# A two-layer transformer block on one core: 122 positions of its time table changed

## What is computed

```python
xn = layernorm(x)
# layer 0: latent attention and a mixture of experts
lat = layernorm(xn @ W_dkv) * gamma + beta          # latent of 32
q, k, v = rope(xn @ W_q), rope(lat @ W_uk), lat @ W_uv   # 16 heads of 8
a = causal_softmax(q @ k.T / sqrt(8)) @ v @ W_o
gates = softmax(top2_of_8(xn @ Wg + bg))
f = sum(gates[e] * (relu(xn @ W1[e] + b1[e]) @ W2[e] + b2[e]) for e in range(8))
x = x + a + f
xn = layernorm(x)
# layer 1: three attentions mixed, and a feed-forward with four matrices
mod = sigmoid(xn @ cg_W + cg_b + cons_vec @ am_W + am_b)     # one per head
ctx = 0.3 * softmax(mod * (q1 @ k1.T) / sqrt(8)) @ v1 + 0.7 * mha(xn, ca, 4 heads)
ctx = 0.85 * ctx + 0.15 * mha(ctx, mc, 4 heads)
h = silu(xn @ w1) * (xn @ w2)
f = gelu(gelu(h @ h1) @ h2) @ w3
x = x + ctx @ Wo + f
```

## Time and profile before

| What | Value |
|---|---|
| Time, three runs | 1737.87, 1743.94, 1736.77 us; median 1737.87 |
| Profiled execution | span 1744.8 us, 34024 instructions |
| PE busy | 1542.1 us (88%), 11497 matmuls |
| PE weight loads (beside matmuls) | 656.0 us (38%) |
| DVE busy | 1199.4 us (69%) |
| ACT busy | 1055.2 us (60%) |
| POOL busy | 792.1 us (45%) |
| Transfers | 159.35 MB, mean 91 GB/s |

### The profile page before, as it was taken

How to read it: one execution, slowest core, us unless ns; L and a number is a source line. 1 busy time by engine, 2 the same in 40 slices (tenths; PEclk the granted TensorE clock), 3 DMA queues, 4 the chain that set the end, 5 groups by cost and what they waited for, 6 DMA issues and landing times.

```text
span 1744.8 us, 34024 instructions
## 1 busy us (share of the span) xinstructions
PE 1542.1 (88%) x11497; PEld 656.0 (38%) x11497; DVE 1199.4 (69%) x3135; ACT 1055.2 (60%) x2322; POOL 792.1 (45%) x725
## 2 busy tenths in 40 slices
PE   3586898999999999998999999999999999889878
PEld 1353453245333543345333543345324533232232
DVE  7554478567875788667885788677876677476523
ACT  2372475667656765676666765677657765636442
POOL 5246345535645456354644455354644461501120
PEclk9998699999999999999999999999999999989877
DMA  7652451136212631136212621145212620201010
GB/s 277 205 153 69 135 158 36 57 109 176 63 34 77 167 102 48 63 115 159 63 34 87 180 79 52 62 135 145 58 46 82 186 78 7 62 15 35 1 37 6
DMA packets 138875, 159.35 MB, mean 91 GB/s; under 512 B 15744, under 2 KB 100304, under 8 KB 137808
## 3 DMA queue, kind: packets, MB, share of 16 engines
q1 hardware_dynamic: 134608, 148.79, 29.4%
q0 software_dynamic: 4096, 8.40, 1.6%
HBM read 115.96 MB, written 40.85 MB: 90 GB/s over the span
## 4 chain that ended last, share of the span: by engine, by line
PE 61%; DVE 13%; ACT 9%; issue 6%; POOL 6%; DMA 3%; SPq 2%; ACTq 0%; POOLq 0%; DVEq 0%
PE banks L454 58%; DVE negmax L879 6%; ACT probs L1222 3%; ACT hm L1291 3%; POOL psums L1443 2%; POOL xslots L1417 1%; DMA qkc<-relm 1%; DVE h L1103 1%; ACT L1222 1%; PE banks L731 1%; POOL halves L1399 1%; PE banks L684 1%; SPq L1579 1%; ACT h L1340 1%; POOL yg L1432 0%
## 5 line engine op out<-in xcount | busy, mean ns | idle before, releaser
L1222 ACT ACTIVATE probs<-banks 128x512 f32<-128x512 f32 (+3 forms) x1216 | 582.1, 535 | 371.7 <-PE banks L454 352.9
L879 DVE TENSOR_REDUCE negmax<-banks 128x1 f16<-128x512 f32 x768 | 492.2, 685 | 159.5 <-PE banks L454 156.5
L875 DVE CUSTOM_DVE_ANT_0 scr<-banks,mask_row 128x384 bf16<-128x384 f32 (+3 forms) x512 | 230.2, 487 | 150.9 <-PE banks L454 149.1
L454 PE MATMUL banks<-kp,qs 32*128 32x512 f16 (+3 forms) x1024 | 239.7, 360 | 60.4 <-DVE negmax L875 23.5
L454 PE MATMUL banks<-probs,vp 128*32 128x512 f32 (+3 forms) x2048 | 241.0, 544 | 0.2 <-POOL probs L1395 0.2
L454 PE MATMUL banks<-qs,kp 32*128 32x512 f16 (+3 forms) x1024 | 218.5, 352 | 23.2 <-ACT probs L1222 15.9
L1483 POOL TENSOR_TENSOR h_lo<-h,h_hi 128x512 f16<-128x512 f32 x96 | 114.4, 1209 | 246.4 <-ACT h_hi L1334 150.8
L1423 POOL TENSOR_TENSOR hl<-hm,hh 128x512 f16<-128x512 f32 x120 | 139.7, 1166 | 131.7 <-DVE hh L1045 131.7
L1291 ACT ACTIVATE hm<-banks,wt 128x128 f32<-128x128 f32 x480 | 137.8, 374 | 77.4 <-PE banks L454 77.0
L454 PE MATMUL banks<-qkc 97*128 97x512 f16 (+1 forms) x512 | 168.5, 402 | 8.7 <-DVE negmax L879 3.0
L454 PEld LDWEIGHTS banks<-kp,qs 32*128 32x128 f16 x1024 | 63.1, 92 | 277.5 <-DVE negmax L879 109.8
(11 more groups left out here) (212 smaller groups left out, 2462.0 us busy)
## 6 DMA issues: line engine op xcount, KB each, us to landing
wt<-wexp SPq DMA_DIRECT2D x120, 258.0 KB, 3.1
wt<-wexp SPq DMA_DIRECT2D x120, 256.0 KB, 3.0
qkc<-relm SPq DMA_DIRECT2D x96, 128.0 KB, 3.2
qs<-relq SPq DMA_DIRECT2D x64, 128.0 KB, 2.3
kp<-relk SPq DMA_DIRECT2D x64, 128.0 KB, 2.3
relm<-halves SPq DMA_DIRECT2D x32, 256.0 KB, 2.1
xg<-xslots SPq DMA_DIRECT2D x24, 256.0 KB, 3.0
yslots<-yv SPq DMA_DIRECT2D x24, 256.0 KB, 3.6
```

The source lines that it names most:

```text
L454: return nc.tensor.matmul(psum[rows_, bank, cols_], lhsT, rhs, start=start, stop=stop)
L875: v.tensor_tensor_reduce(scr[:, s, 0:kw], psum[:, SCO + s, 0:kw], mask_row[:, T - kw:T], -1.0, 3e38, ALU.add, ALU.min, negmax[:, g.n % 2, ...
L879: v.tensor_reduce(negmax[:, g.n % 2, NC * h + c:NC * h + c + 1], psum[:, SCO + s, 0:kw], AX.X, ALU.max, negate=True).then_inc(sem("max"), 1)
L1222: a.activation(keys(g, c)[:, 2 * pair + s, q0:T], psum[:, TRA + s, q0:T], ACT.Exp, scale=SCALE[main(g)]).then_inc(sem("exp"), 1)
```

## The change

122 of the 311 positions in the table change, most by one to three slots, some by more (`x_load` by nine, the last of `spread0`, the query sum and `mc_spread` by six). No step is added or removed, and every wait stays, with its count renumbered from the table. The order inside a slot's body is the same. Two of the last batch's fillers now have positions 767 and 768, behind the end of the loop. The diff is whole, without its header:

```diff
@@ -80,8 +80,9 @@
 PLAN += [("a1", "mid", at, gr) for gr, at in enumerate((120, 128, 136))] + [("a1", "last", 152, NG - 1), ("mc", "tail", 224, 0)]
 A1_AT = (120, 128, 136, 152)
 
-MOVE = {"route": {0: 6}, "warm0": {-1: -6}, "warm1": {-1: 6}, "front": {}, "keys": {0: -8, 1: -5}, "joined": {0: 3}, "prep": {0: 13},
-        "ca": {-1: -24}, "mid": {-1: -24}, "last": {-1: -30}, "ffn": {-1: -24}, "tail": {-2: -12, -1: -52}}
+MOVE = {"route": {0: 6, 1: -1}, "warm0": {-2: 1, -1: -6}, "warm1": {2: 1, -2: -1, -1: 6}, "front": {}, "keys": {0: -8,
+        1: -5}, "joined": {0: 3}, "prep": {0: 13}, "ca": {-1: -24}, "mid": {-1: -24}, "last": {-1: -30}, "ffn":
+        {-1: -24}, "tail": {-2: -12, -1: -52}}
 
 
 @dataclass
@@ -113,57 +114,57 @@
     return out
 
 
-AT = {"l1_split": 14, "x_load": -59, "x_stat": -50, "x_root": -49, "x_norm": -48, "xT0": -39, "xT0_out": -38, "xr_hi": -43,
-      "xr_lo": -42, "lat": -36, "lat_stat": -36, "lat_root": -34, "lat_norm": -33, "latT": -33, "latT_out": -32, "q0": -34,
-      "q0_out": -33, "q0r": -32, "q0r_out": -31, "q0_sum": -30, "q0_send": -27, "k0": -19, "k0_out": -18, "k0r": -16,
-      "k0r_out": -15, "k0_sum": -15, "k0_send": -12, "rank0": -35, "rank1": -32, "rank2": -33, "gex": -33, "gates": -29,
-      "pos": -29, "starts": -27, "slots": -25, "addresses": -25, "pick": -10, "v0a": 3, "v0a_out": 4, "v0b": 30,
-      "v0b_out": 29, "gT": 39, "gT_out": 40, "back0": 53, "back0_out": 54, "wo0": 57, "wo0_out": 58, "x1_stat": 63,
-      "x1_root": 65, "x1_norm": 66, "xT1": 67, "xT1_out": 69, "xl1": 72, "cg": 71, "cg_out": 71, "mod": 72, "q1": 73,
-      "q1_out": 75, "q1_low": 75, "q1_send": 76, "k1": 75, "k1_out": 76, "k1_low": 75, "k1_send": 78, "caq": 77,
-      "caq_out": 78, "caq_low": 79, "caq_send": 80, "cak": 79, "cak_out": 79, "cak_low": 82, "cak_send": 82,
-      "ca_spread": 109, "cav": 112, "cav_out": 113, "v1": 129, "v1_out": 130, "bo": 100, "ca_div": 136, "ca_mul": 141,
-      "ca_o": 143, "ca_o_out": 145, "gelu1": 151, "gelu2": 166, "f3": 171, "f3_out": 173, "f3_add": 172, "back1": 181,
-      "ctx": 181, "mcq": 205, "mcq_out": 205, "mcq_low": 207, "mcq_send": 209, "mck": 208, "mck_out": 209, "mck_low": 210,
-      "mck_send": 213, "mc_spread": 217, "mcv": 220, "mcv_out": 221, "mc_div": 249, "mc_mul": 250, "mc_o": 254,
-      "mc_o_out": 255, "ctx2": 256, "wo1": 256, "wo1_out": 256, "store": 257}
-AT.update({("spread0", i): at for i, at in enumerate((-7, -5, 5, 17), 0)})
-AT.update({("spread1", i): at for i, at in enumerate((110, 117, 126, 142), 0)})
+AT = {"l1_split": 15, "x_load": -50, "x_stat": -46, "x_root": -46, "x_norm": -45, "xT0": -39, "xT0_out": -38, "xr_hi": -44,
+      "xr_lo": -40, "lat": -36, "lat_stat": -36, "lat_root": -35, "lat_norm": -33, "latT": -33, "latT_out": -32, "q0":
+      -34, "q0_out": -33, "q0r": -32, "q0r_out": -31, "q0_sum": -24, "q0_send": -25, "k0": -19, "k0_out": -18, "k0r":
+      -16, "k0r_out": -16, "k0_sum": -15, "k0_send": -11, "rank0": -35, "rank1": -32, "rank2": -33, "gex": -33,
+      "gates": -27, "pos": -27, "starts": -27, "slots": -25, "addresses": -24, "pick": -11, "v0a": 3, "v0a_out": 3,
+      "v0b": 31, "v0b_out": 30, "gT": 39, "gT_out": 40, "back0": 53, "back0_out": 54, "wo0": 57, "wo0_out": 58,
+      "x1_stat": 63, "x1_root": 65, "x1_norm": 66, "xT1": 67, "xT1_out": 69, "xl1": 66, "cg": 72, "cg_out": 72, "mod":
+      74, "q1": 73, "q1_out": 74, "q1_low": 75, "q1_send": 76, "k1": 75, "k1_out": 75, "k1_low": 76, "k1_send": 78,
+      "caq": 77, "caq_out": 78, "caq_low": 80, "caq_send": 79, "cak": 79, "cak_out": 79, "cak_low": 81, "cak_send":
+      81, "ca_spread": 106, "cav": 112, "cav_out": 113, "v1": 129, "v1_out": 131, "bo": 100, "ca_div": 136, "ca_mul":
+      141, "ca_o": 143, "ca_o_out": 144, "gelu1": 152, "gelu2": 166, "f3": 171, "f3_out": 173, "f3_add": 171, "back1":
+      181, "ctx": 181, "mcq": 205, "mcq_out": 205, "mcq_low": 207, "mcq_send": 208, "mck": 208, "mck_out": 209,
+      "mck_low": 210, "mck_send": 209, "mc_spread": 211, "mcv": 220, "mcv_out": 222, "mc_div": 249, "mc_mul": 250,
+      "mc_o": 254, "mc_o_out": 255, "ctx2": 256, "wo1": 256, "wo1_out": 257, "store": 257}
+AT.update({("spread0", i): at for i, at in enumerate((-6, -5, 8, 23), 0)})
+AT.update({("spread1", i): at for i, at in enumerate((106, 117, 127, 143), 0)})
 AT.update({("h0", i): at for i, at in enumerate((28, 36, 43, 51), 0)})
 AT.update({("h0_out", i): at for i, at in enumerate((28, 37, 44, 52), 0)})
-AT.update({("h1", i): at for i, at in enumerate((151, 157, 166, 179), 0)})
-AT.update({("h1_out", i): at for i, at in enumerate((152, 157, 167, 180), 0)})
-AT.update({("up", i): at for i, at in enumerate((9, 12, 13, 16, 17, 20, 22, 24, 25, 29, 30, 32, 34, 35, 38), 0)})
-AT.update({("down", i): at for i, at in enumerate((13, 15, 17, 19, 21, 23, 25, 27, 31, 32, 33, 35, 37, 39, 42), 0)})
-AT.update({("wup", i): at for i, at in enumerate((5, 7, 7, 10, 12, 15, 17, 19, 21, 25, 25, 25, 29, 31, 33), 0)})
-AT.update({("wdn", i): at for i, at in enumerate((9, 11, 13, 15, 17, 19, 21, 23, 25, 27, 29, 31, 33, 35, 37), 0)})
-AT.update({("scatter", i): at for i, at in enumerate((-16, -15, -16, -15), 0)})
-AT.update({("gather", i): at for i, at in enumerate((45, 46, 48, 49), 0)})
-AT.update({("xg_load", i): at for i, at in enumerate((-5, -4, 7, 19), 0)})
+AT.update({("h1", i): at for i, at in enumerate((147, 157, 166, 179), 0)})
+AT.update({("h1_out", i): at for i, at in enumerate((150, 160, 167, 180), 0)})
+AT.update({("up", i): at for i, at in enumerate((9, 11, 13, 16, 17, 20, 22, 24, 25, 29, 30, 32, 34, 35, 38), 0)})
+AT.update({("down", i): at for i, at in enumerate((13, 15, 17, 18, 21, 23, 25, 27, 31, 33, 34, 35, 37, 39, 41), 0)})
+AT.update({("wup", i): at for i, at in enumerate((5, 7, 8, 10, 12, 15, 16, 19, 22, 25, 25, 25, 30, 32, 33), 0)})
+AT.update({("wdn", i): at for i, at in enumerate((10, 11, 13, 15, 16, 19, 20, 23, 25, 27, 28, 31, 33, 34, 39), 0)})
+AT.update({("scatter", i): at for i, at in enumerate((-18, -17, -16, -14), 0)})
+AT.update({("gather", i): at for i, at in enumerate((44, 46, 48, 49), 0)})
+AT.update({("xg_load", i): at for i, at in enumerate((-3, -3, 8, 22), 0)})
 AT.update({("xg", i): at for i, at in enumerate((7, 15, 23, 31), 0)})
 AT.update({("xg_out", i): at for i, at in enumerate((7, 15, 23, 31), 0)})
-AT.update({("y_out", i): at for i, at in enumerate((19, 28, 36, 42), 0)})
-AT.update({("y_store", i): at for i, at in enumerate((20, 29, 37, 43), 0)})
-AT.update({("w_store", i): at for i, at in enumerate((-4, -3, -2, 2), 0)})
+AT.update({("y_out", i): at for i, at in enumerate((18, 28, 35, 41), 0)})
+AT.update({("y_store", i): at for i, at in enumerate((21, 33, 39, 42), 0)})
+AT.update({("w_store", i): at for i, at in enumerate((-3, 1, 1, 2), 0)})
 AT.update({("turn", i): at for i, at in enumerate((72, 6, 47), 0)})
-AT.update({("warm0", i): at for i, at in enumerate((34, 37, 43, 47, 51, 55, 56, 57, 66, 68), 0)})
-AT.update({("warm1", i): at for i, at in enumerate((178, 181, 186, 188, 192, 192, 194, 194, 197, 199), 0)})
+AT.update({("warm0", i): at for i, at in enumerate((37, 37, 51, 49, 51, 56, 61, 61, 67, 68), 0)})
+AT.update({("warm1", i): at for i, at in enumerate((184, 186, 192, 201, 197, 196, 198, 195, 202, 199), 0)})
 AT.update({("scale", i): at for i, at in enumerate((52, 51), 0)})
-AT.update({("split", i): at for i, at in enumerate((-12, -11, -2, 3, 7, 21, 35), 0)})
-AT.update({("load", i): at for i, at in enumerate((1, 14, 25), 4)})
+AT.update({("split", i): at for i, at in enumerate((-17, -17, -8, 2, 6, 19, 33), 0)})
+AT.update({("load", i): at for i, at in enumerate((-1, 11, 24), 4)})
 AT.update({("fa", i): at for i, at in enumerate((133, 135, 137, 139), 0)})
 AT.update({("silu", i): at for i, at in enumerate((134, 136, 138, 141), 0)})
 AT.update({("fb", i): at for i, at in enumerate((134, 136, 138, 141), 0)})
 AT.update({("glu", i): at for i, at in enumerate((135, 137, 139, 142), 0)})
-AT.update({("glu_low", i): at for i, at in enumerate((136, 138, 140, 143), 0)})
+AT.update({("glu_low", i): at for i, at in enumerate((134, 138, 138, 142), 0)})
 AT.update({("g1", i): at for i, at in enumerate((142, 145, 147, 149), 0)})
-AT.update({("hid1", i): at for i, at in enumerate((145, 147, 149, 151), 0)})
-AT.update({("gelu1_hi", i): at for i, at in enumerate((152, 152, 152, 153), 0)})
-AT.update({("gelu1_low", i): at for i, at in enumerate((153, 153, 153, 153), 0)})
+AT.update({("hid1", i): at for i, at in enumerate((144, 147, 149, 151), 0)})
+AT.update({("gelu1_hi", i): at for i, at in enumerate((152, 152, 152, 154), 0)})
+AT.update({("gelu1_low", i): at for i, at in enumerate((151, 154, 154, 155), 0)})
 AT.update({("g2", i): at for i, at in enumerate((155, 158, 161, 164), 0)})
 AT.update({("hid2", i): at for i, at in enumerate((158, 161, 164, 166), 0)})
-AT.update({("gelu2_hi", i): at for i, at in enumerate((167, 167, 168, 168), 0)})
-AT.update({("gelu2_low", i): at for i, at in enumerate((168, 168, 169, 169), 0)})
```

(2 more changed lines are left out.)

## The result

The changed kernel takes 1794.04 us (median of 4 runs, 1783.38 to 1798.62) against 1738.16 us for the kernel before; the ratio is 1.0287, with a 95% interval of 1.0247 to 1.0326. That is 50 us (by the ratio) slower; the quotient of the two medians is 1.032, 56 us. One execution of all, 1950.3 us at a mean clock of 0.733, of the kernel with five groups back, is left out of its figures. The forecast had the direction, but 17 us of it, and the time lies above the range. Lines of the changed file stand one higher than in the file before (L454 is L455).

What follows compares the result with a forecast made beforehand. PE's own queue was taken to set the pace, 2.4 us a slot. Terms 10.5 + 12 + 4 - 1 - 4.6 + 2 - 7 + 1 gave +17, so 1755 us as a median; 80% range 1728 to 1775.

Steps and rivals of the forecast that it cites:

- Part 1: Last head group's spread, SP 17 to 23: lands late for slot 24's score, 1.5 us in seven batches, +10.5 us.
- Part 2: Input statistics and normalisation on DVE: maxima of slots 35 and 36 begin late, 2.0 us a batch, +12 us.
- Part 3: First gelu and gate projection, slots 71 to 72: the key projection starts 0.6 to 0.8 us late, +4 us.
- Part 4: Last quarter of the values, PE slot 30 to 31: fills a wait, cancelled by a late row of maxima, -1 us.
- part 5: Small fills of PE's waits, including the mix's transfers, -4.6 us; position counts later on PE, a loss of +2 us.
- Part 6: Head, batch 0: weight load and stores before the slot load remove most of a 7.37 us PE wait, -7 us.
- Part 7: Tail: eight filler matmuls move between matmuls of the last batch, +1 us.
- (c): Rival: slower still, 1775 us, as new gaps in each period bring extra half-clock stretches; chance 0.05.
- (b): Rival: no difference, 1740 us; only the spread's or the statistics' loss comes, head and fills pay for it; chance 0.25.
- (a): Rival: faster, 1713 us; the spread lands in 2.2 us and DVE absorbs the statistics; chance 0.18.

Runs made afterwards that it cites:

- five groups back: Changed kernel with gate weights and query sum, last spread, input statistics, mix transfers and last quarter of the values at their old positions: 1758.3 us, ratio 1.0112.
- the gelu's neighbourhood: Kernel before with only the steps around the first gelu and the gate projection moved as in the change: 1735.54 us, ratio 0.9977.

## Why the prediction was off

| Part | Forecast (ends) | Alone, by ratio | In the changed kernel's trace |
|---|---|---|---|
| 1 Last spread | +10.5 (1.4 to 13.5) | +27 | 16.3 us of waits, 7 batches |
| 2 Input statistics | +12 (3 to 15) | +18 | 0.8 us a batch at slot 37 |
| 3 Gelu, gate projection | +4 (-8.7 to 10) | -4 | w: 9.4 to 0.5 us, smaller ones new |
| 4, 5 Values and mix | -3.6 (-9 to 5) | +20 (apart +5, +4) | 15.7 us for the row of maxima |
| 5 Position counts | +2 (0 to 4) | not run | not told apart |
| Gate weights | no term | +11 | 18.4 us of waits, 6 batches |
| 6 Head | -7 (-9 to -3) | -1 | 7.4 away, 4.1 back |

("Alone" is the ratio less one, times 1739. For the fourth row the forecast is part 4 with the mix's 2.6. Part 7, the tail's +1, was not run alone.)

**Part 1, mechanism right, size wrong.** The waiting instruction, the queue and the slot are as foretold, and in batch 5 so was the size: 1.42 us in the changed kernel for the 1.5 forecast. The step that failed is "batches 1 to 7: 7 x 1.5". The sum was worked out on batch 5, as all of them were, since the steady batches repeat the pattern. PE's pattern does repeat, but the transfers' margin doesn't: in the same slot the wait is 3.84 us in batch 4 and 2.99 in batch 1. The mean is 2.3, and alone 2.8, above the upper end of 1.9. What was mis-sized is the time between the issue of the keys and PE being ready for them: 2.0 us in the forecast (984.2 to 986.17), 0.3 to 1.6 and 0.9 in the mean in the changed kernel. The start after the issue, 2.9 to 4.4 and 3.2 in the mean, came out under the 3.5 that the term used. Batch 5 has the widest margin of the seven, so that its 1.42 us for 1.5 is luck. The times say more than the waits: 24 us come back when the move is undone and 27 appear when it is made alone, for 16.3 and 19.6 us of waits; where the rest lies is open.

**The gate weights, a term missing.** The prediction says "most pass nothing that waits" and gives the gate weights' move on DVE (-29 to -27) no term; part 5 looked only at the counts that PE computes for DVE, and not at what the gate weights meet in their new slot. That step failed: 18.4 us of waits stood where nothing was put. There POOL runs three key sums of 2.3 us in a row, and each product ends with one of them. In the kernel before they lasted 0.42 and 0.77 us, where 0.18 was possible, and each ended 0.05 us after a piece of POOL's work there too; the rows were there to be read:

```profile
1044.36 0.42 DVE L987 TENSOR_TENSOR gates<-gates,gex 128x32 f32<-128x32 f32 x1
...
1045.24 0.77 DVE L990 TENSOR_TENSOR gates<-gates,gsum 128x32 f32<-128x32 f32 x1
```

It made the largest new waits of the trace, 3.1 to 3.2 us in five of six batches, and +11 us when moved alone. Not all of that comes back from the changed kernel: with the gate weights in their old slot other waits stand there.

**Part 2 was right in kind and near in size** (+18 for +12, above the end of 15). What its waits for the maxima show is less, 7.7 us over the run, and 1.6 us around slot 37 of batch 5 for the 2.0 forecast; the quickest run of that kernel is the one profiled, and how the rest divides wasn't traced.

**Part 3, wrong side, inside its ends.** The end at which q1's wait goes was counted as "nothing replaces it"; smaller waits did in part: the stretch's waits fell from 2.2 us to 1.7. The tanh does end later and the query projection waits 0.54 us for it, as foretold; the eviction's wait that it was set against was the larger.

**Part 4 and the mix.** The order on SP came out as foretold, and so did the landing: the row of maxima is the new wait. The mix's 2.8 us of waits went, as forecast. The step that failed is "The two cancel: 0": the landing of the row of maxima was bounded at 0 to 1.7 us, and its waits are 1.1 to 2.3 us in seven batches of the changed kernel (11.5 in all) and 4.2 in the last, for seven of 1.0 and one of 2.95 before. Forecast 0 and -2.6; each alone is +5 and +4, together +20. No run separates that further.

**Part 6, wrong.** Stores and load before the slot load was right for the changed kernel, and so was the missing wait at 61 us. "Then the scatters' slots bound it" named the right bound and put it at no cost: beside the stores the scatters themselves end 4 us later, the slot load behind them is issued 5.9 us later, and its wait (7.71 us for 3.58) took back over half of the one removed. With the weights' steps moved alone, a wait of 4.85 us for expert weights took most of the rest.

**Rivals.** (c), extra half-clock stretches from new gaps, had a chance of 0.05 and was priced at 17 us on the forecast. Its kind came: a period's clock fell from 0.99 to 0.97, and behind the 3.14 us wait the rows show the lower level, with PE at 1.00 where the wait is taken away. What it cost isn't shown: in the profiled run PE's busy time is the same 1542 us as before, and the 36 us of the span are all idle time. With the sizes that the changed kernel's trace has for the spread and the gate weights, the forecast would have been about 17 + 6 + 18 = 41 us for the 50 measured; that it comes near is no proof, since parts 3, 4 and 6 were off as well. Not slower and faster, (b) and (a), held 0.43 and were excluded.

**Interaction.** By the ratios, the parts alone add to 4.1% (1.56 + 1.02 + 0.66 + 1.16 - 0.23 - 0.05), about 72 us, against 50. The rest of the table, or the overlap of the parts, gives some 20 back. That undoing the mix's move costs 17 us by the ratios where doing it costs 4, and that the gate weights return into a slot which is no longer free, are two such overlaps that the traces show. With five groups undone 1.1% remains. Its trace names part of that: 17.5 us of waits for the mix's transfers, which those moves themselves brought back, and, at other positions, waits for the second feed-forward eviction (h L1104, 6.8 us for 2.4), one of 3.8 us for 0.3 in the last batch for transfers of its last mix (qkc<-pack), and the slot load's. Which moves make these was not tried, so the loss among the other positions stays open. No version beat the kernel before by more than the gelu's neighbourhood, 0.2%.

## What to carry to other kernels

A table of positions in which many steps moved together can't be judged one step at a time from one batch: read the margin of a moved transfer in every batch, since the engine's pattern may repeat where the transfer's does not. Before a step moves into a new slot, list what the engines beside it do there, not only its own queue. Where PE is the bound, price a new wait at its length, and look at what stands ready to wait in its place when it goes: the gate weights' wait of 18.4 us was gone in three kernels, and their times fell by 10 us at most by the ratios.

## What the runs showed of the hardware

A DVE product of two tensors in SBUF of 128x32 took 0.18 us with nothing on POOL (27.08 us of the kernel before), and 1.67 and 1.83 us in a row of POOL sums of 2.3 us each, ending 0.05 us after a sum. With one operand in PSUM it took 0.19 us beside the same sums; reductions, reciprocals and the copy (0.18 to 0.20) were not stretched either. An operation with one tensor in SBUF and a result there can be: the comparison of 128x32 at 646.04 us of the kernel before (L926) lasted 1.62 us where 0.18 is possible, ending 0.05 us after a piece of POOL's work (646.44, 1.17 us). The Trainium skill ("SBUF — State Buffer", SBUF: two separate sides) states it as an exclusive lock on a port pair that DVE and GpSimd share, which a DVE operation with two SBUF inputs needs against a GpSimd operation that reads SBUF: whichever starts first holds it for its whole instruction, and the other is fully blocked. The traces agree, in the ends of the rows and in the run with the operand moved.

The same transfer of 128 KB, in the same slot and order, let PE wait between 1.1 and 4.1 us in seven batches of one run. The score that reads it started 3.0 to 4.7 us after its issue there, and 2.9 to 4.4 in the changed kernel.

The mean clock of an execution is no measure of its loss. Its median was 0.954 in the kernel before and 0.927 in the changed one, but part of that is one stretch of the head: from 20 to 72 us the profiled executions with the gate weights back and with their operands in PSUM have 0.54 and 0.53, with PE busy for 24 and 25 of the 52 us, and those of the kernel before and the changed one have 1.00. With the last spread back, two executions at 0.945 (1763.6 and 1764.1 us) took the same time as two at 0.927 and 0.928 (1764.2 and 1764.0). The times of one kernel spread by up to 1%. A single profiled run was among the quickest for two kernels (changed: 1783.38 against 1794; input statistics: 1749.22 against 1756), and the spans of the two profiles alone put the change at 36 us.
